# Moving 14 shared-expert pieces behind the routed experts, and one gating product from GpSimd to VectorE

## What is computed

```
logits = x @ gate_weight.T ; 6 of 64 experts per token, from 3 of 8 groups
slot   = flat * C + minimum(pos, C - 1)          # C = 96 rows per expert
buf    = zeros(E*C, H).at[slot].set(x[tok])      # the last row of a full expert is overwritten
g, u   = buf @ Wg.T, buf @ Wu.T                  # M = 176
out    = (silu(g) * u) @ Wd.T
y      = sum over 6 of out[slot] * topk_w
shared = (silu(x @ Sg.T) * (x @ Su.T)) @ Sd.T    # MS = 352, every token
return x + y + shared
```

## Time and profile before

| | |
|---|---|
| median of the runs | 741.9 us |
| the profiled execution, its own time | 745.7 us |
| its span, first to last instruction | 743.9 us |
| busy: PE, DVE, POOL, ACT | 656.2, 473.3, 341.0, 332.9 us |
| mean granted TensorE clock | 0.946 |
| expert loop, first late piece to last down product | 478.6 to 692.9 us |
| from there to the end of the span | 51.0 us |

### The profile page before, as it was taken

The page is one execution under the profiler, slowest core; times in us unless marked ns, Lnnn a source line. Parts: engine busy times, 40 slices in busy tenths (PEclk is TensorE's granted clock), DMA queues, the critical chain, the costliest instruction groups (busy, mean ns, idle before and its releaser), DMA issues. The chain is left out here.

```text
span 743.9 us, 16763 instructions
## 1 busy us (share of the span) xinstructions
PE 656.2 (88%) x6161; PEld 462.8 (62%) x6161; DVE 473.3 (64%) x1275; ACT 332.9 (45%) x634; POOL 341.0 (46%) x377
## 2 busy tenths in 40 slices
PE   1699999999879988899989899699999989999690
PEld 0356666666667766676773366478678768778470
DVE  3166776767779788989874699245445435455246
ACT  2367777776658777767654422122222212222000
POOL 6012222212543344534312364847767757775372
PEclk9899999999999999999999999899999999999655
DMA  8122233355443232222311294159999988843596
GB/s 247 28 62 53 63 83 81 86 103 105 100 103 72 52 77 70 57 51 66 96 37 42 77 267 131 40 145 239 247 222 252 222 218 224 220 72 48 141 342 229
DMA packets 144705, 94.27 MB, mean 127 GB/s; under 512 B 62192, under 2 KB 142320, under 8 KB 144624
## 3 DMA queue, kind: packets, MB, share of 16 engines
q1 hardware_dynamic: 129008, 74.58, 38.3%
q0 software_dynamic: 10240, 14.16, 10.5%
q10 hardware_dynamic: 5376, 4.46, 1.9%
HBM read 60.26 MB, written 24.50 MB: 114 GB/s over the span
## 5 line engine op out<-in xcount | busy, mean ns | idle before, releaser
L1430 POOL DMA_INDIRECT sum_d<-tk,targets x64 | 91.8, 1435 | 45.6 <-DVE tk L1518 29.7
L790 DVE TENSOR_REDUCE mx<-Sc 128x16 f32<-128x1024 f32 x64 | 78.2, 1223 | 37.4 <-PE Sc L434 37.1
L1259 PE MATMUL Sc<-xT,wgu_sb 128*128 128x96 f32 (+1 forms) x768 | 93.3, 271 | 0.0
L658 ACT COPY ET<-ring 128x512 f32<-128x512 f32 x128 | 68.9, 589 | 42.8 <-PE ring L446 40.2
L1259 PEld LDWEIGHTS Sc<-xT,wgu_sb 128*128 128x128 f32 (+1 forms) x768 | 87.8, 188 | 0.4 <-issue 0.4
L462 PEld LDWEIGHTS O<-vbd,ET 128*64 128x64 f32 x2048 | 66.5, 138 | 29.3 <-issue 16.9
L794 DVE TENSOR_TENSOR E<-Sc,mx 128x1024 f32<-128x1024 f32 x64 | 78.4, 1225 | 6.9 <-DVE mx L790 0.5
L446 PE MATMUL ring<-ident,E 128*128 128x128 f32 x512 | 70.9, 283 | 12.3 <-ACT E L697 12.3
L434 PE MATMUL Sc<-kbd,qT 64*64 64x256 f32 x1024 | 73.0, 389 | 4.5 <-DMA kbd<-kT 4.5
L462 PE MATMUL O<-vbd,ET 128*64 128x34 f32 x2048 | 73.6, 225 | 3.2 <-ACT ET L658 2.7
L1506 DVE TENSOR_TENSOR hid<-sil,Sc 64x96 f32<-64x96 f32 x64 | 16.4, 256 | 93.4 <-ACT sil L1355 93.1
(11 more groups left out here) (205 smaller groups left out, 1227.4 us busy)
## 6 DMA issues: line engine op xcount, KB each, us to landing
wgu_sb<-in_wgu_dram SPq DMA_DIRECT2D x128, 176.0 KB, 3.5
sum_d<-zeros SPq DMA_DIRECT2D x16, 524.0 KB, 5.7
kbd<-kT SPq DMA_DIRECT2D x248, 32.0 KB, 2.2
wda_sb<-in_wd_dram SPq DMA_DIRECT2D x32, 160.0 KB
X<-in_x_dram SPq DMA_DIRECT2D x8, 512.0 KB, 6.2
rows_d<-xhT SPq DMA_DIRECT2D x8, 512.0 KB, 3.0
xnT<-sum_d SPq DMA_DIRECT2D x8, 512.0 KB, 8.0
wgu_sb<-sum_d SPq DMA_DIRECT2D x8, 512.0 KB, 8.6
```

The costliest lines, as they stand in the source:

```text
L658: nc.scalar.copy(ET[:, m % 2, 4 * v:4 * v + 4].rearrange("p j q -> p (j q)"), bank(name)[:]).then_inc(s_act, 1)
L790: nc.vector.reduce_max(mx[:, m % 2, :], sc, AX.X).then_inc(s_mx, 1)
L1259: last = nc.tensor.matmul(GP[e % 2][0:m, CAP * u:CAP * (u + 1)], wgu_cols[j][:, c, m0:m0 + m], xT[:, e % 2, c, :], start=c == 0, stop=c == 1)
L1430: pool.indirect_dma_start(w["sums"][e % 2], bass.IndirectOffsetOnAxis(ap=targets[:, e:e + 1], axis=0), outs[:, e % OB, :], None, compute_o ...
```

## The change

Three things. The 40 late pieces are placed anew: none ahead of the loop, 26 in it (groups 4 and 5 whole, the six U of group 6) in steps 1 to 58, and 14 behind it: the four D of group 6 right behind the loop, the six U of group 7 between the two halves of the overflow blocks, the four D of group 7 behind these. The product gate times up of group 3 goes from POOL to DVE, ahead of the masking of `wt` (L1607); POOL gathers three rows' lists at once instead. The overflow ring has six banks instead of eight, DVE adds the DRAM sums of groups 0 to 3 between overflow blocks, and two of eight SBUF areas for the sums move, since group 7's inputs are read longer.

```diff
-    AHEAD = 2
-    SLOTS = {(NE - 1) * (k - AHEAD) // (len(LATE) - AHEAD): k for k in range(AHEAD, len(LATE))}
+    INSIDE = LU[NG - 2, 5] + 1
+    SLOTS = {1 + (NE - 4) * k // INSIDE: k for k in range(INSIDE)}
+    BEHIND = [range(INSIDE, LU[NG - 1, 0]), range(LU[NG - 1, 0], LD[NG - 1, 0]), range(LD[NG - 1, 0], len(LATE))]
+    OVER = 6
@@ tensor
             early_down(GE - 1)
-            for k in range(AHEAD):
-                late(k)
             for e in range(NE + 2):
...
+            for k in BEHIND[0]:
+                late(k)
             pe.wait_ge(s_last, 32)
             pe.wait_ge(s_over, 1)
             pe.wait_ge(s_xe, NE)
             pe.wait_ge(s_o, NE)
-            pe.wait_ge(s_ladd, GT * (NG - GE))
-            for b in range(2 * NG):
...
+            for b in range(NG):
+                overflow(b)
+            for k in BEHIND[1]:
+                late(k)
+            for b in range(NG, 2 * NG):
+                overflow(b)
+            for k in BEHIND[2]:
+                late(k)
@@ gpsimd
-            hidden(GE - 1)
             pool.wait_ge(s_list, 1)
-            for e in range(2):
+            for e in range(3):
                 gather(e)
             add(GE - 2)
-            for e in range(2, XB):
+            for e in range(3, XB):
                 gather(e)
             add(GE - 1)
@@ vector
+            dve.wait_ge(s_hid, 3 * (GE - 1))
+            dve.wait_ge(s_dn, 2 * (GE - 1))
+            for c, (m0, m) in enumerate(MC):
+                dve.wait_ge(s_sil, silus(GE - 1, 2 * c + 1))
+                nc.vector.tensor_tensor(hT[0:m, c, :], sg[0:m, c, :], su[0:m, c, :], ALU.mult).then_inc(s_hid, 1)
+
             dve.wait_ge(s_thr, 2)
             dve.wait_ge(s_tk, 1)
             nc.vector.scalar_tensor_tensor(out=wt[:], in0=tk[:], scalar=thr[:], in1=wt[:], op0=ALU.is_lt,
...
+            for k in BEHIND[0]:
+                late_drain(k)
+            dve.wait_ge(s_add, GE)
+            for b in range(NG):
+                overflow(b)
+            for k in BEHIND[1]:
+                late_drain(k)
+            for g in range(2):
+                result(g)
+            for b in range(NG, 2 * NG):
+                overflow(b)
+                if b % 4 == 3:
+                    result(b // 4)
+            for k in BEHIND[2]:
+                late_drain(k)
+            for g in range(4, NG):
+                result(g)
```

More of the change, by code:

```diff
@@ L1058, in moe_phase @@
     wgu_words = wgu[:].rearrange("p j n -> p (j n)")
-    y1 = [wgu_words[:, GT * E * g:GT * E * (g + 1)].rearrange("p (t e) -> p t e", e=E) for g in range(NG)]
+    free = [wgu_words[:, GT * E * g:GT * E * (g + 1)].rearrange("p (t e) -> p t e", e=E) for g in range(NG + 2)]
+    y1 = free[0:NG]
+    y0 = [free[NG + g // (NG // 2)] if g % (NG // 2) == NG // 2 - 1 else y0[:, g] for g in range(NG)]
     wgu_cols = [wgu[:, j, :].rearrange("p (c n) -> p c n", c=2) for j in range(EB)]
@@ L1188, in _ @@
             for g in range(NG):
-                sp.dma_start(y0[:, g], sums[0][g]).then_inc(s_y[g], 16)
+                sp.dma_start(y0[g], sums[0][g]).then_inc(s_y[g], 16)
                 sp.dma_start(y1[g], sums[1][g]).then_inc(s_y[g], 16)
@@ L1295, in _, with overflow @@
                     down_pair((e - 3) // 2)
+            def overflow(b):
+                if b >= OVER:
+                    pe.wait_ge(s_xo, b - OVER + 1)
+                for t in range(2):
+                    at = 256 * (b % NG) + 128 * t
+                    rows = weight_rows(NG + b // 2)
+                    last = nc.tensor.matmul(P[b % OVER][:, E * t:E * (t + 1)], wt[rows, at:at + 128], lastsb[rows, :],
+                                            start=True, stop=True)
+                last.then_inc(s_ov, 1)
+            for k in BEHIND[0]:
+                late(k)
             pe.wait_ge(s_last, 32)
@@ L1361, in _ @@
             save_down(GE - 1)
-            for k in range(AHEAD):
-                late_silu(k)
             for e in range(NE + 1):
@@ L1370, in _ @@
                     silu(e - 1)
+            for pieces in BEHIND:
+                for k in pieces:
+                    late_silu(k)
             for g in range(NG):
@@ L1477, in _ @@
                 pool.wait_ge(s_y[g], 32)
-                nc.gpsimd.tensor_tensor(y0[:, g], y0[:, g], y1[g], ALU.add).then_inc(s_sum, 1)
+                nc.gpsimd.tensor_tensor(y0[g], y0[g], y1[g], ALU.add).then_inc(s_sum, 1)
         @block.vector
@@ L1492, in late_drain @@
                     dve.wait_ge(s_late, k + 1)
+                    if g == NG - 1:
+                        dve.wait_ge(s_xo, 2 * NG)
                     nc.vector.tensor_tensor(x, out[:, 0:E], x, ALU.add).then_inc(s_ladd, 1)
@@ L1608, in _ @@
                                            op1=ALU.mult).then_inc(s_over, 1)
-            for k in range(AHEAD):
-                late_drain(k)
             for e in range(NE + 2):
@@ L1623, in overflow, with result @@
             def overflow(b):
+                g = b // 2
                 dve.wait_ge(s_ov, b + 1)
+                if GE <= g < NG - 1:
+                    dve.wait_ge(s_ladd, GT * (g - GE + 1))
                 xt = X[:, 2 * b:2 * b + 2, :]
[L1626 to L1632, removed]
+                nc.vector.tensor_tensor(xt, P[b % OVER][:].rearrange("p (t e) -> p t e", e=E), xt,
+                                        ALU.add).then_inc(s_xo, 1)
+            def result(g):
                 dve.wait_ge(s_sum, g + 1)
                 dve.wait_ge(s_xo, 2 * g + 2)
+                if g == NG - 1:
+                    dve.wait_ge(s_ladd, GT * (NG - GE))
                 x = X[:, GT * g:GT * (g + 1), :]
-                nc.vector.tensor_tensor(x, x, y0[:, g], ALU.add).then_inc(s_res, 1)
+                nc.vector.tensor_tensor(x, x, y0[g], ALU.add).then_inc(s_res, 1)
+            for k in BEHIND[0]:
[15 more added lines that the diff above has]
+                result(g)
 def decoder_layer(nc, x, ctx_rows, wq, bq, wk, bk, wv, bv, wc, bc, gate, sgu, sd, wgu, wd, out):
```

## The result

The changed kernel takes 719.3 us (median of four executions, 712.2 to 720.9), the kernel before 741.9 in the same comparison: ratio 0.967, interval 0.963 to 0.970. The profiled execution took 718.9, its span is 717.0. The forecast was 717.5, range 708 to 730.

The account below looks back on a forecast made before the run. PE, almost without a break in the expert loop, was taken as the bound. Last down product 27.9 us earlier, end section 3.5 longer: -24.4 from the median 741.9 gives 717.5; own range 710 to 723, with rivals 708 to 730.

Parts of the forecast that it names:

- T': End of the last down product, from which the end section is counted; forecast at 665.0, 27.9 us earlier than 692.9.
- the tail: From the end of the last down product to the kernel's end: 54.5 us against 51.0, +3.5; bounds 46.5 to 59.
- Gate times up on DVE: Ahead of the expert loop: group 3's three products on DVE let PE start its downs 3.15 us sooner.
- Rival (c): Ahead of the loop: the three products wait behind POOL's gathers, losing 2.3 of 3.15 us; time 720, chance 0.07.
- The loop: Expert loop on PE: six U and eight D leave (21.1 us), a stall goes (3.7); 214.2 becomes 189.4 us.
- the stall at 608: In the loop, a D too close behind its group's last U made PE wait; its removal saves 3.7 us.
- POOL is as long as PE: In the loop: POOL needs 2.98 us an expert, PE 2.96; last scatter at 668 to 672, moving the sums only.
- rival (e): POOL paces a loop that does not shrink; no place for more than +6 us; chance 0.04 within the range.
- Rival (b): In the loop the DMA becomes the bound at 239 GB/s: +5.4 us, time 723; chance 0.13.
- Rival (d): In the loop scatters chain on landings of 6.6 us throughout; slower than before, 742 and more, say 746; chance 0.05.
- The clock: Behind the loop: PE's clock was taken to hold through the overflow blocks, a block about 0.87 us instead of 1.71.
- rival (a): PE's clock falls at the overflow blocks or in the short wait before the last downs: +8.4 us, time 726; chance 0.16.

Follow-up runs that it names:

- the masking moved: Changed kernel with the masking of `wt` moved from behind DVE's three products to DVE's third step of the loop; 714.0 us, ratio 0.959; run again 716.3, 0.961.
- the moved D: Changed kernel with the four D of group 6 moved from right behind the loop to behind the first half of the overflow blocks; 727.7 us, ratio 0.979.

## Why the prediction was right, and where its steps were off

The forecast's sum was -24.4 us on the span. Counted from the token transpose it was -24.3 (254.1 against 278.4) and -25.3 in the second trace. The span itself fell by 26.9, of which 2.6 lie ahead of the token transpose, in code that the change leaves alone. Two terms of the sum were off in opposite directions: T' came 1.6 to 2.5 us later than forecast, the tail was 2.4 to 2.5 us shorter. That the sum came out within 1 us is luck to that extent.

**Gate times up on DVE.** Right in its own terms: 0.63 us a product, downs 2.8 us behind the token transpose, half clock again, -3.17 against -3.15. Wrong was what stands beside it. Rival (c) asked whether gathers hold the products; the products and the masking held the gather. I had looked at who waits for DVE's work and not at what DVE's work locks out, although the port rule stood in the text. Its price is a wait of PE of 1.5 us, the same within 0.01 us in all six traces that have the product and the masking on DVE ahead of the loop and no U ahead of the first transposes. At the first scatter it is 1.7: 21.9 us behind the token transpose, against 20.2 in the three traces with the masking moved and 20.5 forecast (486 less 465.5). From the token transpose to the end the two traces of each kind differ by 1.0 to 3.1. The Trainium skill ("SBUF — State Buffer", SBUF: two separate sides) describes a DMA issued by GpSimd that is held up while a DVE operation has the shared port pair, and names a perf-mode operation as the case. Here it was operations with two SBUF operands, and the trace agrees with the rest: 5.22 us against 1.21.

**The loop.** From the first transposes to T' the forecast was 189.4; after shows 192.2 and its second trace 191.4, or 190.0 and 189.9 without the waits of 1.5 us and, in the first, 0.7. The version with the masking moved has 189.6 and 189.9, the one with the product on POOL 189.6. So the prices of U, D and the steps and the removal of the stall at 608 were right, and what is missing is the held gather's 1.5 us and, in one trace, the 0.7 for which POOL was late. T' came 25.4 and 26.3 us earlier by the yardstick instead of 27.9.

**POOL and DMA.** The warning that POOL is as long as PE was right, and closer than I took it. Forecast for the train of scatters was 183.7 us (669.7 less 486); 184.4 to 187.1 was measured in every kernel with 20 to 26 pieces inside. The last scatter started at T' + 7.1, at the edge of the T' + 3 to 7 that I gave. With 20 and 23 pieces inside POOL paces, so rival (e) was close: at 26 the two engines are about level. Rival (b) fell: windows with 252 and 256 GB/s and PE full show that 239 was no ceiling, as the 254 of the earlier trace rows already had. Rival (d) fell as a price: POOL's waits for landed scatters in the whole loop are 8.2 us, against 4.1 before. Its mechanism shows most plainly in the last nine steps, behind the last gather: every second scatter waits some 0.9 us for a landing, and a step is 1.82 us instead of the 1.74 forecast. The trace of after does not record when a scatter lands, so the forecast's sign of being wrong, landings over 6 us, can only be bounded: each scatter waits for the landing of the one two ahead, and starts two ahead stand 5.9 us apart on average (twice 187.1 / 63), so the average landing is not longer.

The line of the scatters, with its waits:

```profile
L1443 POOL DMA_INDIRECT sum_d<-tk,targets x64 | 91.9, 1435 | 29.9 <-issue 14.4 <-DMA sum_d<-tk,targets 8.2 <-DVE tk L1532 4.6
```

**The clock.** Held, as forecast, and the moved D show why; with the wait uncovered and the clock lost together, 9.5 us of tail were lost, where rival (a) alone was priced at 8.4. The wait of 4 us ahead of the last two D and their half clock did not come: PE stood 1.04 us, as DVE was sooner done.

**The tail.** The term that was mis-sized: +3.5 forecast, +1.1 and +1.0 measured, and by another chain. I let DVE's adds of sums cost 10 us for four; they cost 2.85 for the first two and 1.21 each for the others, 5.3 in all. DVE is through its drains at 702.1, T' + 37 instead of 45. Then it waits for sums 6 and 7, which I had counted as done by then: I had them 3.2 us apart, as before, and they stand 3.9 apart (680.80 to 707.81). Adds and sums that overlap cost time on either side: before, an add that began 0.1 us behind a sum took 3.36 us; here three sums that began behind an add took 3.34, 3.02 and 2.64 instead of 2.34, 2 us in all. From the start of the last scatter to the end it is 45.0 to 45.5 us in all five traces of kernels that have the changed one's order behind the loop and all its stores, with 10.9 MB moved between 680 and 710:

```profile
DMA packets 10923, 10.88 MB, mean 363 GB/s; under 512 B 326, under 2 KB 10921, under 8 KB 10921
```

The sum of the loads of two DRAM tensors and the eight stores, 24 transfers of 512 KB, is 12.6 MB, 35 us at that rate (an estimate from these rows). Storing groups 0 to 3 early, between the loads, is a part that I priced at nothing; without these stores the tail is 3.3 us shorter.

**What stays open.** From the first scatter to T' it is 179.1 to 180.1 us in all seven traces with 26 pieces inside, whenever the first scatter came; so what the held gather costs lies ahead of the first scatter. How much of it the total keeps, 1 to 3 us, rests on two traces of each kind. The 3.3 us of the stores rest on one trace, as do the 4.5 us of DVE's adds between the overflow blocks, which were not undone by themselves in the changed kernel.

## To carry to other kernels

When a loop's bound is taken away, compute the next engine's own train, first to last, in advance: 26, 23 and 20 pieces gave the same 184 to 187 us of scatters, and the pieces taken out beyond 26 lengthened the tail by more than they took from the loop. Work placed in a wait can earn twice if it keeps the clock up for what follows; check what stands right behind the wait. Before work is moved to an idle engine, list what that engine's operations lock out (here the list of POOL's gathers), and in a tail add up the bytes as well as the chain.

## What was unexpected in the hardware

An indirect gather issued by POOL takes 0.93 us, 1.21 the first time, but 5.22 when DVE runs three products and a masking of two SBUF operands at that time: it ends 1.09 us behind the last of them. Behind the products alone it took 2.35. The masking itself took 2.34, the three products 1.88; beside POOL's products, in the kernel before, the masking took 2.71.

Under the same overflow blocks the clock stayed at whichever level it had: 64-row products, fully busy at the half clock, did not raise it in 24 us, and they kept the full clock from 670 to 677 and from 688 to 695, where 128-row products stood ahead of them. Each block then took 0.86 us instead of 1.71.
